# Multi-head attention over 2,048 short sequences: the two halves of the probability transposes are separated on TensorE, and share one PSUM bank

## The reference, cut to what matters

```python
# x: (2048, 64, 128) fp32; four weights (128, 128); HEADS = 4, ATT_D = 32
q, k, v = (split_heads(einsum('bfe,ed->bfd', x, W)) for W in (W_query, W_key, W_value))
scores = einsum('hbqd,hbkd->hbqk', q, k)
attn = softmax(scores, axis=-1)
out = einsum('hbqk,hbkd->hbqd', attn, v)          # heads joined again to 128 columns
out = relu(out + einsum('bfe,ed->bfd', x, W_res))
```

## Time and profile before

| | |
|---|---|
| time, median of 3 runs | 1569.93 us (1569.81 to 1570.12) |
| time of the profiled execution | 1570.47 us |
| its span (first to last instruction) | 1568.7 us |
| TensorE's mean granted clock | 0.998 of full speed |
| busy: PE / DVE / POOL / ACT | 1546.8 / 1392.5 / 1270.0 / 1094.8 us |
| DMA | 135.40 MB, 86 GB/s over the span |

### The profile page before, as it was taken

The page is one execution under the profiler, slowest core; times in us unless marked ns, Lnnn a source line. Parts: engine busy times, 40 slices in busy tenths (PEclk is TensorE's granted clock), DMA queues, the critical chain, the costliest instruction groups (busy, mean ns, idle before and its releaser), DMA issues.

```text
span 1568.7 us, 77760 instructions
## 1 busy us (share of the span) xinstructions
PE 1546.8 (99%) x32768; PEld 1416.5 (90%) x32768; DVE 1392.5 (89%) x1793; ACT 1094.8 (70%) x1794; POOL 1270.0 (81%) x1804
## 2 busy tenths in 40 slices
PE   7999999999999999999999999999999999999997
PEld 6999999999999999999999999999999999999996
DVE  6989898989898989899989898989898989898995
ACT  4777777777777777777777777767676767676765
POOL 4888888888888888888888888888888888888887
PEclk9999999999999999999999999999999999999999
DMA  3444444444444444444444444444444444444442
GB/s 65 92 86 89 86 88 87 88 87 88 88 87 87 88 87 87 87 87 87 87 87 87 88 87 87 87 88 87 87 88 87 88 87 88 88 87 88 87 89 61
DMA packets 677306, 135.40 MB, mean 86 GB/s; under 512 B 545888, under 2 KB 677216, under 8 KB 677216
## 3 DMA queue, kind: packets, MB, share of 16 engines
q1 hardware_dynamic: 675840, 134.30, 41.5%
q10 hardware_dynamic: 1376, 0.26, 0.1%
HBM read 67.37 MB, written 67.11 MB: 86 GB/s over the span
## 4 chain that ended last, share of the span: by engine, by line
PE 98%; POOL 1%; issue 0%; DVE 0%; DMA 0%; ACTq 0%; ACT 0%; POOLq 0%
PE ps_so L243 18%; PE ps_pt L234 17%; PE ps_so L223 14%; PE ps_qk L199 12%; PE ps_qk L200 8%; PE ps_vr L212 8%; PE ps_qk L201 8%; PE ps_vr L213 8%; PE ps_vr L214 8%; POOL y L155 0%; POOL y L161 0%; DMA w_raw<-in_L_rec_W_res_dram 0%; ACTq L332 0%; POOL v_diag L170 0%; POOLq L40 0%
## 5 line engine op out<-in xcount | busy, mean ns | idle before, releaser
L155 POOL TENSOR_TENSOR y<-attn,vr 128x256 f32<-128x256 f32 x512 | 386.1, 774 | 168.9 <-POOL v_diag L170 164.5
L170 POOL COPY v_diag<-vr 64x264 f32<-64x264 f32 x1024 | 415.8, 406 | 103.9 <-POOL y L161 40.6
L307 ACT COPY probs_t<-ps_pt 128x512 f32<-128x512 f32 x512 | 274.9, 589 | 306.2 <-PE ps_pt L234 306.2
L161 POOL TENSOR_SCALAR y<-y 128x512 f32<-128x512 f32 x256 | 462.0, 1805 | 22.4
L362 DVE TENSOR_REDUCE row_max<-ps_so 128x16 f32<-128x1024 f32 x256 | 313.5, 1225 | 122.0 <-PE ps_so L223 122.0
L292 ACT COPY qk<-ps_qk 128x512 f32<-128x512 f32 x512 | 300.7, 587 | 118.9 <-PE ps_qk L201 98.9
L199 PE MATMUL ps_qk<-x_hi,w_hi 128*128 128x256 f32 x1024 | 338.0, 330 | 11.0 <-DVE x_lo L353 9.8
L299 ACT COPY vr<-ps_vr 128x512 f32<-128x512 f32 x512 | 298.9, 584 | 32.9
L367 DVE TENSOR_TENSOR shifted<-ps_so,row_max 128x1024 f32<-128x1024 f32 x256 | 313.5, 1225 | 8.8
L243 PE MATMUL ps_so<-v_diag,probs_t 128*64 128x66 f32 x8192 | 296.4, 224 | 2.8 <-POOL v_diag L170 2.5
L212 PE MATMUL ps_vr<-w_hi,x_hi 128*128 128x256 f32 x1024 | 290.0, 283 | 0.7 <-ACT vr L299 0.7
(11 more groups left out here) (21 smaller groups left out, 1702.5 us busy)
## 6 DMA issues: line engine op xcount, KB each, us to landing
x_in<-in_r_x_dram SPq DMA_DIRECT2D x1024, 64.0 KB, 2.2
out_dram<-y SPq DMA_DIRECT2D x256, 256.0 KB, 2.3
w_raw<-in_L_rec_W_query_dram ACTq DMA_DIRECT2D x1, 64.0 KB, 2.4
w_raw<-in_L_rec_W_key_dram ACTq DMA_DIRECT2D x1, 64.0 KB, 2.6
w_raw<-in_L_rec_W_value_dram ACTq DMA_DIRECT2D x2, 32.0 KB, 2.7
w_raw<-in_L_rec_W_res_dram ACTq DMA_DIRECT2D x2, 32.0 KB, 2.7
```

The lines of the kernel that those rows point to most:

```text
L155: nc.gpsimd.tensor_tensor(y[:, n % 2, a * HALF:(a + 1) * HALF].rearrange("k t (p j d) -> k j (t p) d", j=2, d=D), attn[:, n % 2, a * HALF: ...
L161: nc.gpsimd.tensor_scalar(y[:, n % 2], y[:, n % 2], 0.0, None, ALU.max).then_inc(y_ready, 1)
L170: nc.gpsimd.tensor_copy(v_diag[n % 2][j * F:(j + 1) * F, seq, :, :, :, j].rearrange("k a t p d -> k a (t p) d"), vr[n][seq * F:(seq + 1) * ...
```

## The change

Three things change together. On TensorE the transposes of half 1 move from directly behind those of half 0 to the place between v/residual of half 0 and q/k of half 1. On ACT the copy of half 1 moves likewise, from behind the copy of half 0 to between `copy_vr` half 0 and `copy_qk` half 1. And `ps_pt` becomes one bank, used by both halves in turn, so each half's transposes wait until the other half's copy has read the bank; one of the eight PSUM banks stays unused.

```diff
-        ps_qk, ps_vr, ps_pt = banks("ps_qk"), banks("ps_vr"), banks("ps_pt", 2)
+        ps_qk, ps_vr, ps_pt = banks("ps_qk"), banks("ps_vr"), banks("ps_pt")
...
             def transpose_probs(i, a):
-                if has(i - 1):
-                    pe.wait_ge(pt_ready, halves(i - 1, a))
+                if a == 1 or has(i - 1):
+                    pe.wait_ge(pt_ready, halves(i, a) - 1)
                 for t in range(HALF):
                     for p in range(PAIRS):
...
-                        last = nc.tensor.transpose(ps_pt[:, a * BANK + c * P:a * BANK + (c + 1) * P], pair, ident[:, :])
+                        last = nc.tensor.transpose(ps_pt[:, c * P:(c + 1) * P], pair, ident[:, :])
...
                     pe.wait_ge(probs_ready, i)
                     transpose_probs(i - 1, 0)
-                    transpose_probs(i - 1, 1)
                 if has(i + 1):
                     project_qk(i + 1, (n + 1) % RING, 0)
                 if has(i):
                     project_vr(i, n, 0)
+                if has(i - 1):
+                    transpose_probs(i - 1, 1)
                 if has(i + 1):
                     project_qk(i + 1, (n + 1) % RING, 1)
...
-                nc.scalar.copy(probs_t[:, a].rearrange("p c q -> p (c q)"), ps_pt[:, a * BANK:(a + 1) * BANK]).then_inc(pt_ready, 1)
+                nc.scalar.copy(probs_t[:, a].rearrange("p c q -> p (c q)"), ps_pt[:, :]).then_inc(pt_ready, 1)
...
                 if has(i - 1):
                     copy_pt(i - 1, 0)
-                    copy_pt(i - 1, 1)
                 if has(i + 1):
                     copy_qk(i + 1, 0)
                 if has(i):
                     copy_vr(i, n, 0)
+                if has(i - 1):
+                    copy_pt(i - 1, 1)
                 if has(i + 1):
                     copy_qk(i + 1, 1)
```

## The result

The changed kernel takes 1515.91 us (median of 4 runs, 1515.81 to 1516.01), the kernel before 1569.99 us (median of 4 runs). The ratio is 0.9656, with a 95% interval of 0.9639 to 0.9672. The profiled executions are 1516.01 us with a span of 1514.2, and 1570.47 us with a span of 1568.7.

What follows compares the result with a forecast made beforehand. TensorE was taken as the bound, with a hidden 0.22 us stall a step at the single q/k bank. 254 steps at 0.22 give 55.9 us: profiled 1570.47 becomes 1514.6, median 1514 us; range 1508 to 1531.

Steps and rivals of the forecast that it cites:

- What bounds the kernel: TensorE's list sets the time; 0.22 us a step is lost before q/k of half 1, waiting for the single bank `ps_qk`.
- the load itself is no longer hidden: Weight load of q/k of half 1: 0.06 of the 0.22 us, besides 0.16 of waiting for ACT's qk copy.
- 254 steps lose 0.22 us each: Main term of the sum: the stall before q/k of half 1 goes in every counted step, 55.9 us in all.
- the end moves with TensorE: End of the run: POOL's and DVE's last groups shift along with TensorE; steps 0 and 256 are not counted.
- The boundary from v/residual to transposes: TensorE, L214 of half 0 to the moved transposes: taken as 0 extra, with 0.15 us as upper bound.
- A: Boundary v/residual to transpose costs 0.06 us a step, as scores to transposes does: 1529 us; chance 0.15.
- A2: Boundary v/residual to transpose costs 0.15 us a step: 1552 us; chance 0.06.
- D: TensorE drains at the boundary into the moved transposes, 0.30 lost against 0.22 won: about 1590 us; chance 0.04.
- The slacks: Spare time in the new step: 0.26 us for L199's load, DVE some 0.22 left, POOL 0.42 left.
- Rival B: DVE becomes the bound, its 5.58 us chain stretching by 5% to 5.86 in the shorter step: 1527 us; chance 0.06.
- Rival C: The wait at q/k of half 1 stays because ACT's `copy_qk` is late, the 0.22 us returns: 1570 us; chance 0.02.
- Cost nothing: New wait for the one transposes' bank: half 1 has slack 0.64 us; next step's half 0 waits until about 3.2, due 5.80.

## Why the prediction was right

**What bounds the kernel.** Right. TensorE's stream had a hole of 0.22 us a step which the busy share could not show. The runs with none, one and two transposes between give 1570.9, 1543.1 and 1513.4 us, as the cover by time asks.

One reading in it is wrong, though the 0.22 us is right. I split the stall into 0.16 of waiting and 0.06 because "the load itself is no longer hidden". The load ahead of the one that waits, in the kernel before:

```profile
806.00 0.19 PEld L214 LDWEIGHTS ps_vr<-w_hi,x_lo 128*128 128x128 f32 x1
```

The next load was due one distance later, at 806.12, and came at 806.36: 0.24 late. The row says 0.16 only because the record ahead of it lasts 0.19. From a load to the second matmul behind it, it is 0.24 in the stream (805.04 to 805.28) and 0.22 at the stall (806.36 to 806.58), so here being exposed costs nothing on top. The same misreading made the expectation for ACT's old order 0.11 us a step too high.

**The sum.** 1514 was forecast, 1515.9 measured. The term "254 steps lose 0.22 us each" was 55.9 us and is 54.9, or 0.216 a step. Another 0.4 us of the error is what I had left at nothing: the start (0.16, no more than it moves by itself), and the last step, where the single bank costs a wait because no projection lies between. I wrote that the end moves with TensorE; it does, but with 0.22 us more. The remaining half of a microsecond is that the profiled execution and the median lay 0.5 apart before and 0.1 after.

**The boundary from v/residual to transposes.** I took 0 between bounds of 0 and 0.15, by the row with equal tile height. It is 0.12 from L214 to the transpose, an ordinary distance, and the load is hidden. The Trainium skill's rule, in "TensorE: Matmul & The Clock Gate", section "The mechanism", that a load overlaps matmuls in flight only with another row group, is contradicted here again: the transposes' load starts at 806.83, 0.02 after the start of L214, and both use all 128 rows. The same section also lets a load go ahead when it targets the background weight buffer; the traces do not show which buffer a load targets, so that reading stays possible. Rivals A, A2 and D are out.

**The slacks.** L199's load was given 0.26 and has 0.26 (807.00 to 807.26). DVE was given 0.22 and idles 0.23; POOL was given 0.42 and idles 0.44. Rival B is out by 0.2 us, and the run without a projection term shows that DVE is indeed the next in line. Rival C is out, though the run with ACT's old order shows how near it lay: with that one copy in its old place the step grows by 1.42 us.

**The single bank.** "Cost nothing" is right for the 254 steps (1515.9 against 1516.0 with two banks). It rests on the order: in the old one the same bank costs 225 us (1796.3 against 1570.9). The prediction did not say that the stall of 0.22 had a second one behind it, at the v/residual bank; the transposes cover both. A further q/k bank alone did not, in the old order with one bank for the transposes, the only form in which it was tried.

**Open.** Seven kernels with six orders of the same instructions, all without a recorded stall at q/k of half 1, lie between 1511.9 and 1519.4 us. Neither the number of banks (1515.9 and 1516.0) nor the number of boundaries sorts them. The fastest gains its 4 us in distances between projections, several of which are 0.001 to 0.003 us shorter than the 0.120 of the changed kernel. Why they are shorter isn't settled.

## What to carry to other kernels

A pipelined engine at 99% busy can still lose 3.5% in held-back starts: measure from start to start across each wait on a single buffer, and compare with the ordinary distance. If a buffer can't be doubled, put independent work of at least the missing time behind the producer, move the consumer's copy on the other engine to the same place, and check whether the next single buffer in the list has the same hole. Spend on cover only what is missing; here two transposes did what four do.

## What the runs showed of the hardware that was not expected

A stall of TensorE by 0.12 us left no row among the waits, and a row of 0.16 stood for a load that came 0.24 late. The distance between projections of the same shape is 0.120 us in one order and varies between 0.117 and 0.121 in another. A projection put directly behind 32-row tiles costs more than a transpose there: the kernel with that boundary took 1531.4 us against 1516.0. Single transposes spread between projections cost 3.5 us in all against one burst of four. And ACT's copies, each 0.59 us on record, follow one another in 0.48 when queued (804.70 to 805.18 in the run with ACT's old order), so the sum of their records overstates how long a queue of them takes.
